# A hybrid of two attentions and two mixture-of-experts FFNs: the row scatters and gathers of the first FFN in groups of three that wait for landings, and the slot rows of the last two batches computed elsewhere

## The reference, cut to what matters

```python
x = x + _L0_attn_a_ref(_layernorm(x), ...)   # gated attention in groups of 32, with a running state
x = x + _L0_ffn_ref(_layernorm(x), ...)      # this FFN, top 2 of 8 experts
x = x + _L0_attn_b_ref(_layernorm(x), ...)   # 16 heads, softmax over the queries
x = x + _L0_ffn_ref(_layernorm(x), ...)      # the same FFN again

# _L0_ffn_ref
capacity = int(T / E * CAP_FACTOR)                       # 1024 / 8 * 1.25 = 160 slots for each expert
probs = jax.nn.softmax(x @ Wr, axis=-1)
topk_probs, topk_experts = jax.lax.top_k(probs, K)       # K = 2
pos = (running count of earlier choices of the same expert)
keep = pos < capacity
buf = buf.at[e_flat, b_idx, pos_c].add(x_rep * keep)     # tokens into the slots of their expert
h = jax.nn.relu(buf @ W1 + b1)
y = h @ W2 + b2
y_tok = y[e_flat, b_idx, pos_c] * keep * p_flat          # answers back to their tokens
out = y_tok.sum over the K choices
```

## Time and profile before

| | |
|---|---|
| median of 3 runs | 1488.44 us (1484.74 to 1492.68) |
| span of the profiled execution, first to last instruction | 1486.9 us |
| own time of the profiled execution | not listed apart from its span; the span is used |
| first attention, rows 1 to 3 | from about 42 to 137 us |
| experts of m = 1, 2, 3 | 137 to 214 us |
| second attention and what follows | from 214.01 us to the end |
| TensorE busy | 1437.6 us, 97% of the span |

### The profile page before, as it was taken

One profiled execution on the slowest core, in us unless ns is written; L12 is line 12 of the kernel. 1 busy time (PEld: TensorE's weight loads), 2 busy tenths in 40 slices (PEclk: granted clock), 3 DMA queues, 4 the chain that ended last, 5 costly groups with the idle time before them and its releaser, 6 DMA issues.

```text
span 1486.9 us, 43341 instructions
## 1 busy us (share of the span) xinstructions
PE 1437.6 (97%) x18426; PEld 1023.7 (69%) x18426; DVE 1065.3 (72%) x2172; ACT 917.8 (62%) x1727; POOL 280.4 (19%) x325
## 2 busy tenths in 40 slices
PE   7999789999999999999999999999999999999996
PEld 6988774566677675667777756577777565677486
DVE  6884037888666678886766788876666887787754
ACT  5774466666666666566666666666666666666542
POOL 4164613013210012130000120400001214000055
PEclk9999999999999999999999999999999999999999
DMA  8501221001110011010000110110101101101002
GB/s 223 196 20 53 68 65 39 22 23 46 30 29 16 16 42 32 23 48 16 17 16 16 41 32 22 35 33 17 30 16 39 32 23 34 34 16 30 1 19 58
DMA packets 44464, 58.30 MB, mean 39 GB/s; under 512 B 8231, under 2 KB 32656, under 8 KB 44144
## 3 DMA queue, kind: packets, MB, share of 16 engines
q1 hardware_dynamic: 35120, 38.27, 9.4%
q0 software_dynamic: 9152, 17.26, 4.4%
HBM read 22.14 MB, written 19.32 MB: 28 GB/s over the span
## 4 chain that ended last, share of the span: by engine, by line
PE 87%; DVE 5%; ACT 3%; issue 2%; another core or an unknown queue 2%; DMA 0%; DVEq 0%; ACTq 0%
PE bank L1153 29%; PE bank L1166 28%; PE bank L1076 6%; PE bank L1081 4%; PE bank L1090 4%; PE bank L412 2%; PE bank L446 2%; PE bank L1308 2%; PE bank L1304 2%; DVE nmx L1188 1%; PE bank L1265 1%; ACT hT L542 1%; PE bank L830 1%; DVE stats L1349 1%
## 5 line engine op out<-in xcount | busy, mean ns | idle before, releaser
L1197 ACT ACTIVATE prob<-bank,nmx 128x1024 f32<-128x1024 f32 x512 | 570.2, 1114 | 420.3 <-DVE nmx L1188 408.5
L1188 DVE TENSOR_REDUCE nmx<-bank 128x1 f32<-128x1024 f32 x512 | 626.2, 1223 | 200.2 <-PE bank L1153 182.3
L1166 PE MATMUL bank<-prob,vsc 64*64 64x512 f32 x4096 | 644.9, 590 | 1.9 <-DVE ctxT L1215 1.4
L1153 PE MATMUL bank<-q,k 64*64 64x512 f32 x2048 | 527.6, 591 | 3.1 <-ACT prob L1197 1.9
L1153 PE MATMUL bank<-q,ks 64*64 64x512 f32 x2048 | 526.3, 590 | 0.0
L1166 PEld LDWEIGHTS bank<-prob,vsc 64*64 64x64 f32 x4096 | 237.3, 133 | 119.4 <-issue 47.1
L1076 PE MATMUL bank<-xT,wqkv_sb 64*64 64x256 f32 (+1 forms) x1560 | 211.7, 434 | 0.0
L1153 PEld LDWEIGHTS bank<-q,ks 64*64 64x64 f32 x2048 | 139.1, 133 | 75.9 <-issue 21.0
L1760 POOL DMA_INDIRECT yg<-yslots,row_ring x64 | 64.9, 1014 | 609.2 <-PE bank L1153 579.8
L1153 PEld LDWEIGHTS bank<-q,k 64*64 64x64 f32 x2048 | 135.3, 133 | 37.6 <-issue 8.6
L1076 PEld LDWEIGHTS bank<-xT,wqkv_sb 64*64 64x64 f32 x1560 | 92.2, 133 | 86.6 <-issue 36.5
(11 more groups left out here) (270 smaller groups left out, 1628.6 us busy)
## 6 DMA issues: line engine op xcount, KB each, us to landing
ks<-k SPq DMA_DIRECT2D x62, 256.0 KB
yslots<-slots_sb SPq DMA_DIRECT2D x7, 640.0 KB, 3.6
slots_sb<-xslots SPq DMA_DIRECT2D x5, 640.0 KB, 4.5
xslots<-xhat_r POOLq DMA_DIRECT2D x5, 512.0 KB, 7.0
yslots<-xhat_r POOLq DMA_DIRECT2D x5, 512.0 KB, 12.3
w_sb<-in_w SPq DMA_DIRECT2D x1, 2048.0 KB, 9.2
wqkv_sb<-in_wqkv SPq DMA_DIRECT2D x1, 2048.0 KB, 19.0
xslots<-xhat_r,row_s POOLq DMA_INDIRECT x112
```

The source lines that it names most:

```text
L1153: ins = nc.tensor.matmul(bank[rows(c), SC[h][n], :], kk[r, cols(2 * j + c, HD)], qst[pi % 2][r, cols(n, HALF)], start=True, stop=True)
L1166: ins = nc.tensor.matmul(bank[rows(h), CX[n], :], vsc[s][rows(r), rows(h)], prob[g % 3][h][rows(r), cols(n, HALF)], start=(j == 0 and firs ...
L1188: nc.vector.tensor_reduce(nmx[:, 2 * s + h:2 * s + h + 1], bank[:, SC[h][0]:SC[h][0] + 2, :], mybir.AxisListType.XY, ALU.max, negate=True) ...
L1197: nc.scalar.activation(prob[g % 3][h][:].rearrange("p (n c) -> p n c", c=HALF), bank[:, SC[h][0]:SC[h][0] + 2, :], ACT.Exp, bias=nmx[:, 2 ...
```

## The change

Three things are done.

1. The waits on TensorE's progress ahead of scatters and gathers are dropped. In their place, ahead of every third indirect transfer of a batch, GpSimd waits until the transfers issued so far have landed. The landing semaphores are split in two for each batch by the transfer's parity. After 12 of the 16 scatters of m = 1 come the bias of row 3 and place 2; the other four follow.
2. `positions` for m = 3 moves from inside the third expert of m = 1 to the place ahead of its first expert. The wait for `kept_vector` moves with it.
3. m = 2 gets its own table of slot rows, `row_s2`, so place 2 no longer waits for the scatters of m = 1. For m = 3, VectorE writes `row_s` itself, and GpSimd's copy goes.

```diff
-                if e == 5 and m == 1:
+                if e == 2 and m == 1:
                     pe.wait_ge(f_kept, 3)
...
             def beside(e):
-                if e == 3:
-                    positions(pe, 3, POS_F)
                 if e == E - 1:
-                    pe.wait_ge(f_kept, 3)
                     slots_ahead_tensor(pe, 2, slots2, AHEAD[:2])
...
+        def rows_to(m):
+            return row_s2 if m == 2 else row_s
...
-            if m > 1:
-                p.wait_ge(f_sc, 256 * (m - 1))
-            nc.gpsimd.tensor_copy(row_s[:], skip[:]).then_inc(f_idx, 1)
+            nc.gpsimd.tensor_copy(rows_to(m)[:], skip[:]).then_inc(f_idx, 1)
...
-            nc.vector.tensor_tensor(skip[:], rowf[:], skip[:], ALU.add).then_inc(f_plc, 1)
+            for done in f_sc[1]:
+                v.wait_ge(done, 128)
+            nc.vector.tensor_tensor(rows_to(m)[:], rowf[:], skip[:], ALU.add).then_inc(f_idx, 1)
...
             for c in tiles:
                 k, t = c // T, c % T
-                nc.gpsimd.indirect_dma_start(out=xslots[:, :], out_offset=bass.IndirectOffsetOnAxis(ap=row_s[:, k, t:t + 1], axis=0),
+                if c > 0 and c % 3 == 0:
+                    hold(p, f_sc[m][0], 16 * ((c + 1) // 2))
+                    hold(p, f_sc[m][1], 16 * (c // 2))
+                nc.gpsimd.indirect_dma_start(out=xslots[:, :], out_offset=bass.IndirectOffsetOnAxis(ap=rows_to(m)[:, k, t:t + 1], axis=0),
                                              in_=route_rows(m - 1)[:, t, :], in_offset=None,
-                                             bounds_check=B * SLOTS - 1, oob_is_err=False).then_inc(f_sc, 16)
+                                             bounds_check=B * SLOTS - 1, oob_is_err=False).then_inc(f_sc[m][c % 2], 16)
+
+        FIRST = 12
...
             for q in range(4):
                 for k in range(2):
-                    beside_expert(p, 11 + 2 * q + k)
                     for t in (2 * q, 2 * q + 1):
+                        n = 4 * q + 2 * k + t % 2
+                        if n > 0 and n % 3 == 0:
+                            for i in range(2):
+                                hold(p, f_gq[(n - 1 - i) // 4][(n - 1 - i) % 2], 16 * ((n - 1 - i) % 4 // 2 + 1))
...
             place_gpsimd(p, step, 1)
-            scatter_in_attention(p, 1, 3)
-            scatter_in_next(p, 1)
+            hold(p, f_idx, 2)
+            scatter(p, 1, range(FIRST))
+            bias_gpsimd(p, 3)
             place_gpsimd(p, step, 2)
-            scatter_in_attention(p, 2)
-            scatter(p, 2, [13, 14, 15])
-            p.wait_ge(f_plc, 1)
-            p.wait_ge(f_sc, 256 * 2)
-            nc.gpsimd.tensor_copy(row_s[:], skip[:]).then_inc(f_idx, 1)
+            scatter(p, 1, range(FIRST, 2 * T))
+            hold(p, f_idx, 3)
+            scatter(p, 2, range(2 * T))
             hold(p, f_idx, 4)
-            for i in range(8):
-                beside_expert(p, 3 + i)
-                scatter(p, 3, [2 * i, 2 * i + 1])
+            scatter(p, 3, range(2 * T))
             gather(p, step, 1, 0)
...
             pe.wait_ge(f_sub, 4)
+            positions(pe, 3, POS_F)
             experts_tensor(pe, 1, first_batch_tensor(pe), (a_res, 10), following=slots2)
```

More of the change, by code:

```diff
@@ L132, in bass_hybrid @@
         f_kept = sem("f_kept")
-        f_plc = sem("f_plc")
         f_xs, f_ha, f_ya, f_ys = (sem(n) for n in ("f_xs", "f_ha", "f_ya", "f_ys"))
-        f_sc, f_ld, f_st, f_comb = (sem(n) for n in ("f_sc", "f_ld", "f_st", "f_comb"))
+        f_sc = {m: [sem(f"f_sc{m}{i}") for i in range(2)] for m in (1, 2, 3)}
+        f_ld, f_st, f_comb = (sem(n) for n in ("f_ld", "f_st", "f_comb"))
         f_ga = [sem("f_ga0"), sem("f_ga1")]
-        f_gq = [sem(f"f_gq{q}") for q in range(4)]
+        f_gq = [[sem(f"f_gq{q}{i}") for i in range(2)] for q in range(4)]
         f_gb = [sem("f_gb0"), sem("f_gb1")]
@@ L354, in bass_hybrid @@
         row_s = sb("row_s", [P, 2, T], U32, stack=stage_f)
+        row_s2 = sb("row_s2", [P, 2, T], U32, stack=stage_f)
         slots_sb = sb("slots_sb", [P, ST, P], stack=stage_f)
@@ L656, in first_answers_vector @@
             for q in range(4):
-                v.wait_ge(f_gq[q], 64)
+                for done in f_gq[q]:
+                    v.wait_ge(done, 32)
                 for k in range(2):
@@ L669, in scatter @@
                 k, t = c // T, c % T
-                nc.gpsimd.indirect_dma_start(out=xslots[:, :], out_offset=bass.IndirectOffsetOnAxis(ap=row_s[:, k, t:t + 1], axis=0),
+                if c > 0 and c % 3 == 0:
+                    hold(p, f_sc[m][0], 16 * ((c + 1) // 2))
+                    hold(p, f_sc[m][1], 16 * (c // 2))
+                nc.gpsimd.indirect_dma_start(out=xslots[:, :], out_offset=bass.IndirectOffsetOnAxis(ap=rows_to(m)[:, k, t:t + 1], axis=0),
                                              in_=route_rows(m - 1)[:, t, :], in_offset=None,
-                                             bounds_check=B * SLOTS - 1, oob_is_err=False).then_inc(f_sc, 16)
-        def scatter_in_attention(p, m, next_row=None):
-            r = m + 2
-            hold(p, f_idx, m + 1)
-            hold(p, a_vproj, 4 * r + 4)
-            scatter(p, m, [0])
-            hold(p, a_lktr, 2 * r + 2)
-            scatter(p, m, [1])
-            hold(p, a_sq, 2 * r + 2)
-            scatter(p, m, [2])
-            for h in range(2):
-                hold(p, a_sl, 2 * r + h + 1)
-                scatter(p, m, [3 + h])
-            for k in range(2):
-                hold(p, a_kv, 4 * r + 2 * k + 1)
-                scatter(p, m, [5 + k])
-            for k in range(4):
-                hold(p, a_o, 4 * r + k + 1)
-                scatter(p, m, [7 + k])
-                if k == 1 and next_row is not None:
-                    bias_gpsimd(p, next_row)
-            for h in range(2):
-                hold(p, a_out, 2 * r + h + 1)
-                scatter(p, m, [11 + h])
-        def scatter_in_next(p, m):
-            r = m + 3
-            hold(p, a_xproj, 2 * r + 2)
-            scatter(p, m, [13])
-            for k in range(2):
-                hold(p, a_gproj, 4 * r + 2 * k + 2)
-                scatter(p, m, [14 + k])
-        def beside_expert(p, i):
-            hold(p, f_h, E + i + 1)
+                                             bounds_check=B * SLOTS - 1, oob_is_err=False).then_inc(f_sc[m][c % 2], 16)
+        FIRST = 12
         def gather(p, step, m, b):
@@ L1415, in f_norm_vector @@
                 else:
-                    v.wait_ge(f_sc, 256 * (B - 1))
+                    for done in f_sc[B - 1]:
+                        v.wait_ge(done, 128)
                 xhat_vector(v, c0, fb, xhat_r, piece - 5, g_xhat)
@@ L1992, in _ @@
                     store_slots(sp, 1, 0)
-                hold(sp, f_sc, 256 * m)
+                for done in f_sc[m]:
+                    hold(sp, done, 128)
                 hold(sp, f_ld, 16 * m)
```

7 lines of the change are left out of this document (4 added, 3 removed).

## The result

The changed kernel takes 1507.46 us (median of 4 runs, 1505.72 to 1510.06), the kernel before on the same chip 1490.11 (4 runs, 1484.74 to 1492.68). The ratio is 1.0126, 95% interval 1.0105 to 1.0146: slower by 1.26%, and above the range of 1485 to 1505. The span goes from 1486.9 to 1506.6 us.

What follows compares the result with a forecast made beforehand. TensorE was taken as the bound, with the second attention's start set by GpSimd's transfer chain. That start 7.9 us later plus 2 us of low clock gave 9.9, a span of 1496.8 and median of 1498 us; range 1485 to 1505.

Steps and rivals of the forecast that it cites:

- Rival A: GpSimd's group waits: restart hidden beside the landing, gaps 1.1 us for scatters and 1.6 for gathers; faster, 1481 us; chance 0.14.
- B: GpSimd's chain: place 2 takes 4.8 us, loads disturb nothing, gathers land in 1.4; slower but under 0.5%, 1494; chance 0.25.
- D: TensorE's holes stay despite groups of three; it reaches the norm at 212, not 207; same time; chance 0.45 with the forecast.
- signs of being right: Gaps 2.1 and 2.5 us, m = 3 scatters ending near 177, last gather near 210, TensorE idle before L498, `xT_r` wait under 2.
- rival C: Group waits: gathers take 3.0 us per gap, scatters 2.3, 4.7 us more, with 7 us of low clock; 1504; chance 0.10.
- 2 us of low clock: TensorE after idling for the norm: 4 us of low clock fall on the work after, costing 2 us more.
- Kept for m = 2 at 103.9: Ahead of place 2: `kept` for m = 2 ready at 103.9 us, and the bias, ending at 103.1, fits before it.
- Gap of 2.1 for scatters: GpSimd ahead of every third scatter: landing plus restart takes 2.1 us, 5.7 us for a group of three.
- Gap of 2.5 for gathers: GpSimd ahead of every third gather: 1.6 us landing plus 0.9 restart, 6.2 us for a group of three.
- 1 us for loads beside: During the gathers: 1 us added for loads and stores of 640 KB beside them, so landing at 213.0 instead of 212.0.
- holes of the kernel before: TensorE in the first FFN, during back-to-back transfers: 14 to 20 us of holes ready to close; gain hidden under GpSimd's chain.
- +7.9 us of the forecast: Start of the second attention, L1048: at 221.9 us against 214.01, 7.9 us later through GpSimd's chain.

Runs made afterwards that it cites:

- e9_window: Changed kernel with each indirect transfer waiting for the landing of the third before it, instead of group waits: 1466.65 us, ratio 1.0026, calm chip.
- e5_again: Second run of the changed kernel with group waits ahead of the scatters only, none ahead of the gathers: 1484.10 us, ratio 1.0147, calm chip.
- e3_six: Changed kernel with groups of six transfers instead of three: 1471.03 us, ratio 1.0052, calm chip.
- e3_again: Second run of the changed kernel with groups of six instead of three, on another calm chip: 1469.83 us, ratio 1.0054.
- e2_bias: Changed kernel with the bias of row 3 after the eighth scatter of m = 1 instead of the twelfth: 1493.3 us, ratio 1.021, calm chip.
- e7_store_late: Changed kernel with SyncE's store of the fourth batch's slots held until all gathers have landed: 1506.16 us, ratio 1.0141, late chip.
- after_again: The changed kernel once more, unchanged, on a calm chip: 1496.91 us, ratio 1.0228 to the kernel before.
- e1_again: Changed kernel without the group waits of scatters and gathers, run again on a late chip: 1522.44 us, ratio 1.0254.
- before_again: The kernel before once more, unchanged, on a calm chip for its trace: 1462.36 us in the run traced.
- e4_places: Changed kernel keeping moved positions and split tables, with the earlier spreading waits and GpSimd order put back: 1458.53 us, ratio 0.9969, calm chip.
- e5_scatter_waits: Changed kernel with group waits ahead of the scatters only, none ahead of the gathers: 1483.65 us, ratio 1.0138, calm chip.
- e6_gather_waits: Changed kernel with group waits ahead of the gathers only, none ahead of the scatters: 1469.72 us, ratio 1.0048, calm chip.
- e1_no_waits: Changed kernel without the group waits of scatters and gathers: 1459.01 us, ratio 0.9971, calm chip.

## Why the prediction was wrong, by its own steps

**What was right.** The chain that decides is the one named: group waits, scatters of m = 3, gathers, norm, L498. TensorE idles ahead of it for more than 10 us (13.34), the wait for `xT_r` is gone, and the slots of both batches come late for TensorE. Rival A is refuted for the changed kernel, since the waits cost 2.0 us and more. So is B: place 2 took 6.0 us (108.21 to 114.22) and no gather wait was under 2.48. D didn't come to pass, since 1.9 of the 34.9 us of late semaphores were left. Of the signs of being right, two failed: the scatters of m = 3 ended at 185.4 for 177, and the last gather at 221.5 for 210. In rival C, which gave 1504, the mechanism was closest, and it was still 3.5 short.

**Where the 10 us came from.** L1048 was forecast at 221.9, or 223.9 with 2 us of low clock. It was at 234.18, 10.3 later:

- *Start of the row, 1.9 us, no step of the forecast.* Place 1 is at 74.83 for 72.87, ahead of anything changed. In the later profiles it is at 72.8 (e9_window) to 75.5 (e5_again), and for one and the same kernel at 74.67 (e3_six) and 73.16 (e3_again), so this varies from run to run.
- *Kept for m = 2 at 103.9: a missed term, 2.3 us.* The step took the bias ahead of place 2 as free. It landed on VectorE's top 2 selection and held one operation for 2.9 us. e2_bias shows this with 3.2 us at place 2, 2.9 of it from the bias. Place 2 itself was right within 0.3.
- *Gap of 2.1 for scatters: mis-sized, 4.2 us.* The ten waits in m = 2 and m = 3 average 2.60 us. Four are as forecast (2.03 to 2.14); the rest are 2.48 to 3.42, the longest three (3.21 ahead of 128.57, 3.42 ahead of 160.87, 3.21 ahead of 173.18) beside SyncE's 640 KB transfers, issued at 122.74, 154.91 and 168.10; the last has a fetch in it too. The batches take 32.1 and 32.6 us from first scatter to the next step for 29.8 and 30.7.
- *Gap of 2.5 for gathers and 1 us for loads beside: mis-sized, 2.4 us.* The five gaps sum to 15.8 us. The stretch from the first gather to the last add is 37.0 us for 34.6.
- *The rest,* from the last add to L1022, took 10.6 us for 10.9 with the low clock. The 2 us for the clock were right.

1.9 + 2.3 - 0.3 + 4.2 + 2.4 - 0.3 = 10.2. The step that failed is the pricing of a wait: 2.1 us for scatters, 2.5 for gathers and 1 us in all for the large transfers beside them. It was taken from small transfers that were alone. In the changed kernel five of the fifteen waits in m = 2, m = 3 and the gathers lie beside a 640 KB transfer, and they take 17.6 us (3.21, 3.42, 3.21, 2.87, 4.91) for 11.3, so 6.3 over where 1 was put down; a fetch is in two of the five, too. The other ten take 24.2 us for 22.2. (The transfers of the two scatter batches took 0.8 us less than put down, which is why the two lines above add up to less.) Here are the third scatter wait of m = 3 and the transfer beside it, from the timelines of GpSimd and of SyncE's queue:

```profile
173.18 0.97 POOL L676 DMA_INDIRECT xslots<-xhat_r,row_s  x1 [3.21 <-DMA xslots<-xhat_r,row_s]
...
168.10 0.36 SPq L706 DMA_DIRECT2D yslots<-slots_sb  x1
```

e9_window points the same way: the five waits that stand are those beside such transfers. That the large transfer itself makes the landing late isn't shown by taking one away; the one run that moved one (e7_store_late) gained 0.1 us against after_again.

**What was right for a wrong reason.** The holes of the kernel before were taken as a fixed property of back-to-back issue, with about 17 us to be closed. On the late chips that holds: group waits close them (e7_store_late against e1_again). On the four calm chips there are none to close, with 36 scatters and 16 gathers back to back. There the group waits cost 37.9 us and give nothing. The +7.9 us of the forecast are counted from a start of the second attention at 214.01, which on a calm chip is at 197.25 (before_again), while the changed kernel starts it at 234.18 and 233.38. So GpSimd's chain, the part that was worked out, hardly depends on the chip; what it is measured against does. On a calm chip the same chain is a loss of 34.6 us. The forecast's +9.9 us would have been 25 us off there; that it came within 10 us of the measurement is luck of the chip.

**Left open.** Why semaphores come late on some chips isn't known. No waits, 68.5 us late; the order of before, 34.9; groups of three, 0 to 1.9: density of issue goes with it. Whether three in flight without draining (e9_window) is enough there, and what e3_six, e4_places, e5_scatter_waits and e6_gather_waits do, was not seen, since none of these runs fell on such a chip. The part behind the start of the second attention takes 1272.9 us on the late chip and 1262.9 on a calm one, for the same kernel before, and the traces show most of this in the last 60 us, where GpSimd issues its last scatters and gathers back to back. The first of these scatters (L1820) is issued 2.4 us later than on the calm chip, counted from the start of the second attention, the last gather (L1760) 7.2 us later, and ScalarE has another late semaphore in between, where it waits 5.89 us for TensorE on the calm chip:

```profile
1475.17 0.88 ACT L1868 ACTIVATE answers<-bank,slot_owner 128x128 fp32r<-128x128 f32 x3 [9.69 <-remote]
```

The best version for calm chips is e4_places or e1_no_waits (both 0.997); on the late ones nothing that was run there beats the kernel before.

## What to carry to other kernels

Waiting for a whole group of DMAs to drain costs the landing and a restart each time, here 2 to 5 us for every 3 to 4 us of issue; a window that waits for the third transfer before cost nothing at 47 of 52 transfers, and 7.6 us in all on a calm chip. Price each such wait with the large transfers that another queue will send at that moment. Before explaining holes in a profile by the order of the code, see whether they are there on another chip.

## What the runs showed of the hardware that was not expected

- A 128x64 VectorE operation with two inputs in SBUF took 2.91 us (3.17 in after_again) beside GpSimd's 128x1024 addition, for 0.23 without.
- An instruction fetch of 16 KB that falls into a wait, with no large transfer near, goes with 3.48 and 3.65 us for 2.05 (scatters) and 3.22 for 2.75 to 2.85 (gathers); a 640 KB transfer alone goes with 3.13 to 3.58 us for scatters.
- On a late chip, while GpSimd issues indirect transfers every 1.3 us without a break, TensorE starts 29 matmuls in 17.6 us for 152 on a calm one, and of 68.5 us of late semaphores 50.9 end 1.6 to 2.9 us after such a run has ended (e1_again).
- The same program differs by 1.6 to 1.9% between chips (1462.5 for 1486 and 1490 us), with "remote" waits in the stretches of dense indirect transfers on the slower ones alone. The change's ratio is 1.0126 on one kind and 1.0228 on the other.
